# Flamingo block on one core: rounding x for chunks 1 to 3 on GpSimd instead of VectorE

## What is computed

```python
x = x + tanh(g_xattn) * xattn(layernorm(x), ctx, ctx, Wq, Wk, Wv, Wo, bo, masks)
x = x + tanh(g_ffn) * ffn(layernorm(x), ...)
# in ffn:
scale = sigmoid(clip_x) * max(abs(x)) / 127          # one number for all of x
xq = clip(round(x / scale), -128, 127) * scale
gate, up = xq @ fake_quant(w_gate).T, xq @ fake_quant(w_up).T
h = act_fake_quant(silu(gate) * up, clip_down)       # again one maximum over all of h
return h @ fake_quant(w_down).T
```

## Time and profile before

| | us |
|---|---|
| median of three runs | 248.92 (248.47 to 249.05) |
| the profiled execution, its time | 250.41 |
| the profiled execution, its span | 248.8 |
| mean granted TensorE clock in it | 0.956 |
| busy: PE, DVE, ACT, POOL | 210.6, 207.0, 160.5, 133.3 |

### The profile page before, as it was taken

One profiled execution on the slowest core, in us unless ns is written; L12 is line 12 of the kernel. 1 busy time (PEld: TensorE's weight loads), 2 busy tenths in 40 slices (PEclk: granted clock), 3 DMA queues, 4 the chain that ended last, 5 costly groups with the idle time before them and its releaser, 6 DMA issues.

```text
span 248.8 us, 5433 instructions
## 1 busy us (share of the span) xinstructions
PE 210.6 (85%) x1712; PEld 146.9 (59%) x1712; DVE 207.0 (83%) x417; ACT 160.5 (64%) x296; POOL 133.3 (54%) x235
## 2 busy tenths in 40 slices
PE   6699979979979999999999999989834989846940
PEld 6578868858746676666676767656422433314830
DVE  3388888978898998989999999964977689998990
ACT  2255487466597777787887776767624688838900
POOL 7446567642462343577585948437846444320880
PEclk9999999999999999999999999999995799995996
DMA  6989889999646553555555342000004200000594
GB/s 219 271 224 307 267 259 235 268 242 247 162 128 147 129 137 105 130 128 130 128 114 125 88 120 73 1 4 0 3 1 133 78 0 1 3 1 0 59 148 139
DMA packets 34186, 30.82 MB, mean 124 GB/s; under 512 B 5232, under 2 KB 27760, under 8 KB 34160
## 3 DMA queue, kind: packets, MB, share of 16 engines
q1 hardware_dynamic: 29776, 27.74, 41.5%
q0 software_dynamic: 1360, 1.31, 4.5%
q10 hardware_dynamic: 3024, 1.44, 2.1%
HBM read 20.65 MB, written 9.70 MB: 122 GB/s over the span
## 4 chain that ended last, share of the span: by engine, by line
PE 46%; DVE 18%; ACT 10%; issue 9%; POOL 7%; DMA 4%; SPq 3%; ACTq 0%; POOLq 0%; DVEq 0%
PE bank_o L1468 10%; PE bank_a L1451 9%; PE bank_b L1437 7%; PE bank_a L1345 6%; PE bank_a L1477 5%; ACT arena L795 4%; DMA qk_parts<-arena 3%; DVE h_max L1220 3%; DVE big L1229 2%; DVE arena L1257 2%; PE bank_o L1356 2%; DVE v_all L1263 2%; POOL big L492 1%; PE bank_a L1318 1%; DVE x_rows L1279 1%
## 5 line engine op out<-in xcount | busy, mean ns | idle before, releaser
L935 DVE TENSOR_REDUCE neg_max<-bank_b 128x2 f32<-128x512 f32 x128 | 80.2, 676 | 4.7 <-PE bank_b L1334 3.0
L1451 PE MATMUL bank_a<-big 98*128 98x256 bf16 x256 | 48.9, 273 | 3.9 <-ACT arena L795 2.3
L1437 PE MATMUL bank_b<-big 96*128 96x256 bf16 x224 | 42.7, 272 | 0.2 <-issue 0.2
L795 ACT ACTIVATE arena<-bank_a 128x512 f32<-128x512 f32 x64 | 34.2, 606 | 9.8 <-PE bank_a L1451 9.8
L795 ACT ACTIVATE big<-bank_a 128x512 f32<-128x512 f32 x64 | 33.7, 598 | 9.4 <-PE bank_a L1451 9.2
L1451 PEld LDWEIGHTS bank_a<-big 98*128 98x128 bf16 x256 | 20.9, 97 | 20.4 <-issue 7.7
L1345 PE MATMUL bank_a<-arena,w_t 128*128 128x256 f32 x128 | 30.2, 381 | 1.9 <-DVE resid L940 1.3
L1345 PEld LDWEIGHTS bank_a<-arena,w_t 128*128 128x128 f32 x128 | 23.2, 190 | 5.2 <-issue 2.5
L516 POOL TENSOR_TENSOR arena<-resid,arena 128x512 bf16<-128x512 f32 x16 | 18.2, 1156 | 10.9 <-ACT arena L711 10.9
L1437 PEld LDWEIGHTS bank_b<-big 96*128 96x128 bf16 x224 | 21.2, 97 | 4.2 <-DVE neg_max L935 0.8
L873 ACT ACTIVATE arena<-bank_b,w_scale_x 128x512 f32<-128x512 f32 (+1 forms) x24 | 16.1, 686 | 5.8 <-PE bank_b L1606 1.9
(11 more groups left out here) (185 smaller groups left out, 432.9 us busy)
## 6 DMA issues: line engine op xcount, KB each, us to landing
qk_parts<-arena SPq DMA_DIRECT2D x8, 768.0 KB, 5.0
big<-qk_parts SPq DMA_DIRECT2D x32, 192.0 KB, 3.3
big<-qk_parts SPq DMA_DIRECT2D x32, 128.0 KB, 3.3
x_rows<-in_x SPq DMA_DIRECT2D x8, 256.0 KB, 5.3
big<-qk_parts SPq DMA_DIRECT2D x32, 64.0 KB, 3.6
big<-in_ctx SPq DMA_DIRECT2D x7, 256.0 KB, 5.2
out<-x_rows SPq DMA_DIRECT2D x7, 256.0 KB, 3.0
out<-v_all POOLq DMA_DIRECT2D x5, 256.0 KB, 6.3
```

What stands on the lines that cost most here:

```text
L795: act.activation(probabilities(h), ring_bank(b, ("exp", h)).rearrange("p (c s) -> p c s", c=QC), ACT.Exp, scale=SCALE).then_inc(exp_done, 1)
L935: dve.tensor_reduce(neg_max[:, p, :, h], bank.rearrange("p (c s) -> p c s", c=QC), axis=AX.X, op=ALU.max, negate=True).then_inc(max_done, 1)
L1437: done = mm(to, q_st[0:KR, p, h, c * P:(c + 1) * P], k_st[0:KR, p, h], start=True, stop=not masked)
L1451: done = mm(to, k_st[0:KM, p, h, k * P:(k + 1) * P], q_st[0:KM, p, h], start=True, stop=not masked)
```

## The change

GpSimd rounds chunk 1 and copies it into bf16 as soon as the scale is there (`quantise(1)`), with no wait for chunk 0's halves any more. Between its products of h it then rounds chunk 2 and 3 (after its product for c = 1 of chunks 0 and 1) and copies them (after its product for c = 4 of chunks 0 and 1). VectorE keeps only its share of chunk 0. The semaphore is split: `xq_half` counts the halves of chunk 0, `xq_ready` the later chunks.

```diff
+            def quantise(n):
+                over_scale(n)
+                pool.wait_ge(pool_x, n)
+                pool.tensor_copy(xq_b[:, n], x_int[:, n]).then_inc(xq_ready, 1)
+
             pool.wait_ge(scale_ready, 1)
-            pool.wait_ge(last_hat, 1)
-            pool.wait_ge(xq_ready, 2)
-            over_scale(2)
-            over_scale(3)
+            quantise(1)
             for n in range(NCH):
                 for m, c in enumerate(POOL_CHUNKS):
...
+                    if n < 2 and m == 0:
+                        if n:
+                            pool.wait_ge(last_hat, 1)
+                        over_scale(n + 2)
+                    elif n < 2:
+                        pool.wait_ge(pool_x, n + 2)
+                        pool.tensor_copy(xq_b[:, n + 2], x_int[:, n + 2]).then_inc(xq_ready, 1)
...
-            def quantise_ahead():
-
-                for n in (2, 3):
-                    dve.wait_ge(pool_x, n - 1)
-                    whole_x(n)
...
-            chain.step(dve.tensor_scalar(x_int[:, 1].rearrange("p t e -> p (t e)"), hats(1), INV_X, None, ALU.mult))
-            whole_x(1)
...
-                    if first and c == 0:
-                        quantise_ahead()
...
-                    pe.wait_ge(xq_ready, n + 2)
+                    pe.wait_ge(xq_ready, n)
...
-                    pe.wait_ge(xq_ready, half + 1)
+                    pe.wait_ge(xq_half, half + 1)
```

More of the change, by code:

```diff
@@ L283, in flamingo_block @@
         poison_sum, x_over_scale, last_hat = sem("poison_sum"), sem("x_over_scale"), sem("last_hat")
-        xq_ready, xq_tr, xq_t_ready = sem("xq_ready"), sem("xq_tr"), sem("xq_t_ready")
+        xq_half, xq_ready, xq_tr, xq_t_ready = sem("xq_half"), sem("xq_ready"), sem("xq_tr"), sem("xq_t_ready")
         pool_h_done, up_copied, pool_x = sem("pool_h_done"), sem("up_copied"), sem("pool_x")
@@ L1194, in whole_x @@
             def whole_x(n, t=slice(0, CT)):
-                dve.tensor_copy(xq_b[:, n, t], x_int[:, n, t]).then_inc(xq_ready, 1)
-            def quantise_ahead():
-                for n in (2, 3):
-                    dve.wait_ge(pool_x, n - 1)
-                    whole_x(n)
+                dve.tensor_copy(xq_b[:, n, t], x_int[:, n, t]).then_inc(xq_half, 1)
             chain.step(dve.tensor_scalar(x_int[:, 0, 0:2], v_all[:, 0:2], INV_X, None, ALU.mult))
@@ L1221, in h_maximum, with products @@
                                              apply_absolute_value=True))
-            def products(n, first=False):
+            def products(n):
                 for c, maxima_of in zip(DVE_CHUNKS, ((), (0,), (2, 1), (3,))):
@@ L1233, in products @@
                         h_maximum(n, m)
-                    if first and c == 0:
-                        quantise_ahead()
                 h_maximum(n, IC - 1)
                 h_maximum(n, 4)
-            products(0, first=True)
-            for n in range(1, NCH):
+            for n in range(NCH):
                 products(n)
```

## The result

The change costs 1.5 us: 250.41 us median (250.19 to 250.86, five runs) against 248.92 (247.78 to 249.44, five runs), a ratio of 1.0072 with an interval of 1.004 to 1.0103. The forecast was 250.2, within 249.3 to 251.3. The ratios leave out the few executions in which the chip showed a slower state, and they are not the quotients of the medians (250.41 / 248.92 is 1.006).

What follows compares the result with a forecast made beforehand. At the start the end of chunk 0's two copies counts, not VectorE's load; then VectorE and ScalarE alternate every 6.6 us. Freed work 0, start +1.3, loop 0 on 248.92 made 250.2 us, range 249.3 to 251.3.

Steps and rivals of the forecast that it cites:

- VectorE's freed work is worth nothing: Chunk 0: the 3.6 us taken off VectorE are covered by its waiting for silu; gain 0.
- The two engines take turns: Start: GpSimd's instructions hold VectorE's two copies of chunk 0, ending 0.81 and 1.61 late; likeliest case, chance 0.57.
- the forecast's branch of 192.8: Start: VectorE's small tensor_scalar goes behind GpSimd's copy, so the second copy of chunk 0 ends at 192.8, not 192.64.
- the rule that the forecast cited: Trainium skill: of VectorE's SBUF copies, casts, tensor_scalar and GpSimd, whichever starts first holds the port pair for its whole instruction.
- The first product: TensorE at the start: first product at 193.15 to 193.30 instead of 191.93, 1.2 to 1.4 us late, 1.3 taken.
- GpSimd's copy of int8 to bf16: Copy of chunk 1: no row shows it; bounds 0.69 and 2.54 us, 0.98 taken.
- The loop: Chunks 1 and 2: GpSimd's copies reach TensorE 0.55 us late, but silu waits for VectorE anyway; cost 0, period 6.6.
- the cover that the forecast named: Loop: 0.25 us of slack before block 3's silu hides GpSimd's copy; gone at a copy of 1.3 us.
- The clock: TensorE's clock rise moves with the work, 0; if fixed, the delay is halved, 0.65; up to 0.25 may come back.
- Not slower: Rival: engines don't exclude each other, stores of x slowed the copy; first copies keep 0.43, time 248.9; chance 0.13.
- Shared rate: Rival: both engines run together, each slower; copies take 0.94, first product 0.6 later, 249.4 to 249.8; chance 0.16.
- Slow copy on GpSimd: Rival: GpSimd's copy takes 1.3 to 2.5 us, costing at the start and in chunks 1 and 2; 250.6 to 254; chance 0.14.

Runs made afterwards that it cites:

- e1: Changed kernel, but GpSimd waits for both halves of chunk 0 before rounding chunk 1; 248.77 us against 248.45 before, ratio 1.0013.
- e2: Kernel before with only chunks 2 and 3 rounded and copied by GpSimd, chunk 1 left on VectorE; 248.41 us against 248.45, ratio 0.999.
- e5: Changed kernel, but GpSimd waits for the first half of chunk 0 only; 248.65 us against 249.62 before, ratio 0.9947.
- e9: The kernel of e5 measured a second time; 249.25 us against 249.19 before, ratio 1.0008.
- e11: Changed kernel with the changes of e5 and e7 together; 248.21 us against 249.19 before, ratio 0.9962.
- e3: Kernel before with chunk 1 moved to GpSimd at once, chunks 2 and 3 rounded right behind it, copied by VectorE; 250.83 us against 248.45, ratio 1.0112.
- e6: Kernel before with one more GpSimd memset (64 x 1024) right behind the scale; 250.06 us against 249.62, ratio 1.0015.
- e8: The changed kernel measured a second time, beside other kernels; 250.77 us against 249.19 before, ratio 1.006.
- e4: Kernel before with one reduction of 1024 elements on VectorE ahead of its first rounding; 249.88 us against 248.45, ratio 1.0054.
- e7: Kernel before with each chunk's maximum of block 4 moved behind the next chunk's first product; 247.22 us against 249.62, ratio 0.9905.

## Why the prediction was right, point by point

The mechanism held: two turns lost at the start, nothing gained from the freed work, nothing lost in the loop. The total fits better than its parts do, and that is luck: the first product was less late than forecast (1.12 against 1.2 to 1.4), and the clock, forecast to give back 0 to 0.25, took some 0.5 more in the two profiles of the changed kernel.

**VectorE's freed work is worth nothing: right.** VectorE idled 2.97 us before its first product in the changed profile, and 3.28 in e1, against 1.08. e1 and e2 are level with before, and at the same rise of the clock the profiles of e5, e9 and e11 have block 5 where before's has it, to 0.02 us.

**The two engines take turns: right.** Measured from the reciprocal's start, the first copy ends at 1.94 instead of 1.15, 0.79 later (forecast 0.81). The second ends at 3.33 instead of 1.76, 1.57 later (forecast 1.61). The way there differed from the forecast's sum in pieces that cancelled. GpSimd's copy went ahead of the 12-element instruction, as in the forecast's branch of 192.8: its turn came 0.14 sooner than in the sum, and it ran 0.90 (190.82 to 191.72), not 0.98. The second copy then took its full 0.43 and not 0.29, because it waits for the 12-element instruction and no GpSimd instruction was left to hold it once it could start. One part of the rule that the forecast cited isn't borne out everywhere: that the one which starts first goes first holds in the changed kernel, but not by the recorded starts of e3, e6 and the earlier trace rows (the last section has them).

**The first product: 1.12 later, forecast 1.2 to 1.4.** The step was over-sized: the transposes started 0.04 sooner than forecast, and the product started 0.40 us behind the start of the second transposes (192.26 to 192.66), where 0.45 to 0.61 was put.

**GpSimd's copy of int8 to bf16: right within 0.1.** 1.04 alone; bounds were 0.69 and 2.54, the value taken 0.98 behind a turn. The 1.03 cycles an element of the Trainium skill (page "GPSIMD Engine Reference", section 3.1) make an estimate of 0.88 for the elements alone, which fits the 0.90 behind a turn; the row of an undisturbed one is 0.16 longer.

**The loop: right, and right for its reason.** Period 6.62 (and 6.3 at the last boundary, before and after, where the forecast had 6.6 throughout), TensorE's wait for GpSimd 0.33, silu still late because of VectorE. e11 shows the cover that the forecast named: without it the same copy costs 0.18 a chunk.

**The clock: the term that was off, though inside the range.** The forecast set the clock at 0 and left room for 0.25 us to come back. In the two profiles of the changed kernel more was lost instead: block 5 in chunk 0 is 1.73 and 1.66 us later than before while the first product is 1.12 later. Stretches of the changed kernel (busy by engine, granted clock, DMA share, GB/s; rows 8 for before):

```profile
189.00:190.00 1.00, 0.00 (x0) 0.00 (x0) 0.93 (x3) 0.72 (x1) 0.89 (x2) 0.50 0.00 0
190.00:191.00 1.00, 0.03 (x1) 0.06 (x2) 1.00 (x2) 0.00 (x0) 0.93 (x2) 0.50 1.00 324
...
197.00:197.50 0.50, 0.50 (x3) 0.21 (x2) 0.00 (x0) 0.26 (x2) 0.26 (x1) 0.50 0.00 0
...
198.00:199.00 1.00, 1.00 (x12) 0.68 (x11) 0.88 (x2) 0.02 (x1) 1.00 (x2) 1.00 0.00 0
```

The 1.73 us come apart into two pieces. Set at the same rise of the clock (by the formula above the table), block 5 of the four profiles that start late (changed, e8, e3, e4) is 0.62 to 0.64 us later than before, for a first product 1.12 to 1.25 later: about half; in e6 it is 0.43 for 0.85. This is the case that the forecast named and priced at 0.65, a rise that doesn't move with the work. The other 1.1 us is half of 2.2, by which the rise itself was later, 9.13 (e8: 8.99) against 6.92.

By the profiles that late rise isn't mere scatter. Ahead of the scale TensorE sits idle for 4.9 us, and the clock falls to 0.50 at a point that differs between executions. In the two changed profiles it fell 1.11 and 1.25 us ahead of the reciprocal. In e1 and e2, whose first product is on time, it fell 1.18 and 1.15 ahead and rose 5.64 and 5.68 behind it: with the same fall, the late start came with a rise some 3.4 us later. In e3 and e4, as late as the changed kernel, it fell 3.50 and 3.08 ahead and rose at 6.74 and 7.16; of those on time, before, e7 and e11 fell 3.3 to 3.4 ahead and rose at 6.86 to 6.95: there the late start didn't hold the rise back. The quarters of a us in which it fell and rose, in the changed kernel:

```profile
187.75:188.00 0.25, 0.19 (x1) 0.18 (x1) 0.00 (x0) 0.25 (x2) 0.25 (x1) 0.53 0.00 0
...
197.75:198.00 0.25, 0.25 (x3) 0.13 (x2) 0.00 (x0) 0.25 (x1) 0.25 (x1) 0.50 0.00 0
198.00:198.25 0.25, 0.25 (x7) 0.25 (x6) 0.13 (x1) 0.02 (x1) 0.25 (x1) 0.99 0.00 0
```

and in e1 (reciprocal at 188.31):

```profile
187.00:187.25 0.25, 0.00 (x0) 0.02 (x1) 0.11 (x1) 0.25 (x2) 0.25 (x1) 0.76 0.00 0
...
193.75:194.00 0.25, 0.25 (x2) 0.09 (x1) 0.25 (x1) 0.20 (x1) 0.00 (x0) 0.59 0.00 0
```

So by these profiles the late start costs about 0.6 us at block 5 in some executions and 2.4 in others (13.63 against 11.27 in e1), and the medians, 1.5 and 1.6 us slower, would be the mixture. This is argued from a few profiles, one for each kernel. The mean clocks of all executions agree: 0.957 in e8 against 0.959 before, 0.958 in e4 and 0.954 in e3 against 0.960. How often each kind comes up wasn't counted.

**Rivals.** Not slower (the stores of x were to blame): falls, since VectorE's copy was held from its start at 189.59, in a stretch with a DMA share of 0.00 (189 to 190), and since e5's copy kept its 0.43 in a stretch with a share of 1.06. Shared rate: falls with e5, where VectorE's copy kept its 0.43 beside GpSimd. Slow copy on GpSimd: falls with 1.04.

## What to carry to other kernels

In these runs, work moved to GpSimd cost VectorE the rest of GpSimd's instruction whenever that had the turn when a cast or tensor_scalar of VectorE's on the path came up (0.43 became 1.23, 0.23 became 0.99). Read both queues around the narrow place, and keep the wait that holds GpSimd back until the narrow place is passed. Ask of freed work what the engine did next: 3.6 us taken off VectorE where it waits for silu gave nothing, 0.6 us moved in a place where others wait for VectorE gave 0.4 us at each of the first two boundaries and 0.1 at the third. And a step hidden by slack is paid for as soon as another change takes the slack.

## What the runs showed of the hardware

A memset on GpSimd, which reads nothing, held VectorE's tensor_scalar just as a rounding does (1.34 instead of 0.49), and an instruction of only 12 elements was held for 0.99 us instead of 0.23. The recorded starts don't tell who goes first when they are this close: VectorE's copy, 0.04 us ahead, won in e5 (190.52 against 190.56) and in e9; VectorE's copy, 0.07 us behind, won in e3 (191.49 against 191.42); VectorE's rounding, 0.11 us ahead, lost in e6 (188.77 against 188.88), and so did its tensor_scalar of the earlier trace rows, 0.07 ahead (21.04 against 21.11). What decides it stays open. The point at which TensorE gets its full clock scatters from 5.00 to 6.95 us behind the reciprocal between executions in which the first product comes at the same 2.66, and the end of chunk 0 with it, from 10.95 to 11.92: one profile can't tell a change of under 1 us behind such a place, unless the rise of the clock is read too and half its difference taken off.
